# A router of sixteen columns turned round, and a hand-written front put in a new order

## The reference

```python
x = x + attention(layernorm(x), ctx)          # q, k, v projections with biases, softmax over 375 rows
h = layernorm(x)
router_probs = softmax(h @ w_router)          # 8 experts
gate_weights = softmax(h @ w_gating / 0.1)
cw = router_probs * gate_weights
cw = cw / (sum(cw) + 1e-9)
out = x + sum over e of cw[e] * ((silu(h @ w_gate[e]) * (h @ w_up[e])) @ w_down[e])   # 256 -> 1024 -> 256
```

## Time and profile before

| | |
|---|---|
| median of 3 runs | 981.25 us (980.57 to 981.32) |
| profiled execution, its own time | 981.21 us |
| its span | 979.4 us |
| instructions | 16,565 |
| TensorE busy | 971.5 us |
| VectorE, ScalarE, GpSimd busy | 745.7, 482.9, 671.1 us |
| mean granted TensorE clock | 0.999 |

### The profile page before, as it was taken

One profiled execution on the slowest core, in us unless ns is written; L12 is line 12 of the kernel. 1 busy time (PEld: TensorE's weight loads), 2 busy tenths in 40 slices (PEclk: granted clock), 3 DMA queues, 4 the chain that ended last, 5 costly groups with the idle time before them and its releaser, 6 DMA issues.

```text
span 979.4 us, 16565 instructions
## 1 busy us (share of the span) xinstructions
PE 971.5 (99%) x6193; PEld 927.3 (95%) x6193; DVE 745.7 (76%) x1353; ACT 482.9 (49%) x853; POOL 671.1 (69%) x514
## 2 busy tenths in 40 slices
PE   8999999999999999999999999999999999999998
PEld 7999999999999999999999999999999999999998
DVE  6987446877778777788777887777877778777785
ACT  6897554454444444544535444444445454444441
POOL 4799876776757676667667675766766676757642
PEclk9999999999999999999999999999999999999999
DMA  9250140010001010010101010010101010100002
GB/s 227 81 152 20 49 143 23 22 44 16 29 22 44 23 36 30 22 45 22 44 2 43 23 44 22 22 44 23 44 22 32 13 45 22 44 22 23 1 1 76
DMA packets 37352, 40.63 MB, mean 41 GB/s; under 512 B 2644, under 2 KB 35272, under 8 KB 37272
## 3 DMA queue, kind: packets, MB, share of 16 engines
q1 hardware_dynamic: 37264, 39.58, 13.6%
q10 hardware_dynamic: 8, 0.00, 0.0%
HBM read 35.90 MB, written 3.67 MB: 40 GB/s over the span
## 4 chain that ended last, share of the span: by engine, by line
PE 97%; DMA 2%; ACT 0%; SPq 0%; POOL 0%; issue 0%; DVE 0%; DVEq 0%
PE ps L272 94%; DMA shared<-in_ctx 1%; PE ps L1527 1%; PE ps L1615 1%; DMA xf<-in_L_xattn_Wk 1%; PE ps L1555 0%; PE ps L1602 0%; PE ps L1572 0%; PE ps L1516 0%; POOL arena L413 0%; SPq L286 0%; DVE xsacc L1236 0%; ACT arena L647 0%; ACT arena L701 0%; PE ps L1473 0%
## 5 line engine op out<-in xcount | busy, mean ns | idle before, releaser
L272 PE MATMUL ps<-arena 128*128 128x256 f32 (+4 forms) x3120 | 413.7, 284 | 0.2
L272 PEld LDWEIGHTS ps<-arena 128*128 128x128 f32 (+2 forms) x3120 | 403.2, 189 | 6.3 <-POOL arena L480 0.2
L480 POOL TENSOR_TENSOR arena<-shared,arena 128x448 fp32r<-128x448 f32 x196 | 251.0, 1294 | 191.4 <-ACT arena L808 185.6
L272 PE MATMUL ps<-xc_hi,w_hi 128*128 128x448 f32 x904 | 331.9, 367 | 0.0
L272 PE MATMUL ps<-xc_hi,w_lo 128*128 128x448 f32 x904 | 330.2, 365 | 0.0
L272 PE MATMUL ps<-xc_lo,w_hi 128*128 128x448 f32 x904 | 329.7, 365 | 0.0
L801 ACT ACTIVATE shared<-shared 128x448 f32<-128x448 f32 x180 | 101.4, 579 | 192.0 <-DVE shared L1176 125.0
L272 PEld LDWEIGHTS ps<-xc_hi,w_lo 128*128 128x128 f32 x904 | 169.8, 188 | 13.8
L272 PEld LDWEIGHTS ps<-xc_hi,w_hi 128*128 128x128 f32 x904 | 170.6, 189 | 10.2
L272 PEld LDWEIGHTS ps<-xc_lo,w_hi 128*128 128x128 f32 x904 | 170.6, 189 | 10.1
L1170 DVE TENSOR_TENSOR shared<-ps,shared 128x448 f32<-128x448 f32 x60 | 37.5, 625 | 110.8 <-PE ps L272 110.8
(11 more groups left out here) (145 smaller groups left out, 1098.7 us busy)
## 6 DMA issues: line engine op xcount, KB each, us to landing
early<-in_L_ffn_w_down SPq DMA_DIRECT2D x16, 512.0 KB, 4.0
shared<-in_ctx SPq DMA_DIRECT2D x16, 336.0 KB
w_raw<-in_L_ffn_w_gate SPq DMA_DIRECT2D x17, 256.0 KB, 2.9
w_raw<-in_L_ffn_w_up SPq DMA_DIRECT2D x17, 256.0 KB, 3.2
early<-in_L_ffn_w_gate SPq DMA_DIRECT2D x15, 256.0 KB, 2.8
early<-in_L_ffn_w_up SPq DMA_DIRECT2D x15, 256.0 KB, 3.1
x_dram<-xsacc SPq DMA_DIRECT2D x8, 224.0 KB, 3.7
xsacc<-x_dram SPq DMA_DIRECT2D x1, 1792.0 KB, 7.6
```

The lines of the kernel that those rows point to most:

```text
L272: ins = nc.tensor.matmul(dst, w, m, start=first and i == 0, stop=last and i == len(passes) - 1, skip_group_check=onto)
L480: nc.gpsimd.tensor_tensor(h[:, 1, j, at:at + TC], tile, h[:, 0, j, at:at + TC].bitcast(fp32), ALU.subtract).then_inc(hid_lo_done, 1)
```

## The change

The router is computed the other way round. `split_router` (new, VectorE) splits the 16 columns into a high and a low part of fp32r, which lie side by side as 32 columns. `route(cp, c)` (four calls in place of fourteen) takes these 32 columns as the stationary operand and streams a row of 448 tokens past them, for the two halves of the inputs and for `xc_hi` and `xc_lo`: four passes. The result is 32 x 448 in bank 3 or 4. `keep_routed` (new, ScalarE) copies it to SBUF (into a part of `up_t` not yet in use), `transpose_logits(cp)` (new, TensorE) turns it back in seven 128-token pieces to bank 5, and `keep_logits` adds up the part from the high and the part from the low weights. The waits on `logits_done` in `values`, `transpose_norm2` and `down` go; `keep_norm2(4)` no longer waits for `logits_ready`, and the first `quad` waits for both logits.

Beside this, the lists of all five engines before the first `quad` are written in a new order. Nothing is added or taken away there but the router's parts; ten fillers stay ten, placed otherwise: eight before `transpose_weights(1)` where there were five, none in the stretch to `mix_ctx(0)` where there were four, then two where there was one.

```diff
+        wr_split = sb("wr_split", [P, DK, 2, 2 * E], fp32r)
+        lt = up_t[0:4 * E, 0:2, :]
-        ps_l = ps[:, X2_BANK, 0:RT * 2 * E].rearrange("p (i n) -> p i n", i=RT)
+        ps_lt = [ps[0:4 * E, 3 + c, 0:TC] for c in range(2)]
+        ps_l = ps[:, 5, 0:RT * 4 * E].rearrange("p (i l n) -> p i l n", i=RT, l=2)
...
+            load_x(0)
             load_weights(0)
-            load_x(0)
             load_weights(1)
+            load_x(1)
             load_ctx_half(0, 0)
-            load_x(1)
+            load_ctx_half(0, 1)
+            load_router()
             load_wv()
-            load_ctx_half(0, 1)
             load_ctx_half(1, 0)
             load_x(2)
+            load_set(0)
+            load_ctx_half(1, 1)
+            load_ctx(2, 0)
+            load_bv()
             load_x(3)
-            load_ctx_half(1, 1)
-            load_bv()
-            load_set(0)
-            load_ctx(2, 0)
             load_ctx(2, 1)
             load_ctx(3, 0)
+            load_set(1)
...
+            def keep_routed(cp, c):
+                sc.wait_ge(lt_ready, 2 * cp + c + 1)
+                if cp == 0:
+                    sc.wait_ge(cn_lo_done, 2 * PAIRS)
+                else:
+                    sc.wait_ge(logits_ready, 1)
+                nc.scalar.copy(lt[:, c, :], ps_lt[c]).then_inc(lt_kept, 1)
...
# ScalarE's list
             weights_high(0)
+            norm1(0)
             weights_high(1)
-            norm1(0)
+            xt_high(0)
             ct_high(0, 0)
-            xt_high(0)
             cn_high(0, 0)
             m_high()
             ct_high(0, 1)
+            cn_high(0, 1)
             q_high(0)
+            cn_high(1, 0)
             norm1(1)
-            cn_high(0, 1)
+            high_set(0)
             xt_high(1)
+            ct_high(1, 0)
             wv_high()
-            cn_high(1, 0)
-            ct_high(1, 0)
             exponentials(0, 0)
...
# VectorE
+                nc.vector.tensor_reduce(logits[:, cp * RT:(cp + 1) * RT, :], ps_l.rearrange("p i l n -> p i n l"),
+                                        AX.X, ALU.add).then_inc(logits_done, 1)
+            def split_router():
+                ve.wait_ge(router_in, 2 * DMA)
+                nc.vector.tensor_copy(wr_split[:, :, 0, :], wr_raw[:]).then_inc(wr_hi_done, 1)
+                ve.wait_ge(wr_hi_done, 1)
+                low(wr_split[:, :, 1, :], wr_raw[:], wr_split[:, :, 0, :]).then_inc(wr_done, 1)
...
+            stats1(0)
             split_biases()
-            stats1(0)
             weights_low(0)
+            stats1(1)
             weights_low(1)
-            stats1(1)
...
# TensorE
+            def route(cp, c):
+                pe.wait_ge(wr_done, 1)
+                pe.wait_ge(part_lo[cp, "first" if c == 0 else "second"], 1)
+                if (cp, c) == (1, 1):
+                    pe.wait_ge(second7_lo, 1)
...
+                accumulate(ps_lt[c], [(wr_split[:, k - 1, :, :].rearrange("p l n -> p (l n)"), x[:, cp, PLAIN_A[c + 1, k], :])
+                                      for k in (1, 2) for x in (xc_hi, xc_lo)]).then_inc(lt_ready, 1)
+            def transpose_logits(cp):
+                pe.wait_ge(lt_kept, 2 * (cp + 1))
...
+                for i in range(RT):
+                    ins = nc.tensor.transpose(ps_l[:, i, :, :].rearrange("p l n -> p (l n)"), lt_f[:, i * P:(i + 1) * P], ident[0:4 * E, 0:4 * E])
...
             queries(0)
             transpose_ctx(1, 0)
+            scores(0, 0)
             transpose_norm(1)
-            keep_busy(1)
-            scores(0, 0)
             scores(0, 1)
             queries(1)
             transpose_probs(0, 0)
             transpose_ctx(1, 1)
-            keep_busy(1)
-            keep_busy(1)
-            keep_busy(1)
+            scores(1, 0)
             transpose_probs(0, 1)
-            scores(1, 0)
             transpose_ctx(2, 0)
```

More of the change, by code:

```diff
@@ L842, in _ @@
             q_high(2)
+            pt_high(1, 0)
+            norm1(3)
             pt_high(1, 1)
-            norm1(3)
-            high_set(0)
-            ct_high(3, 0)
             at_high(0)
             xt_high(3)
+            cn_high(2, 0)
+            ct_high(3, 0)
+            exponentials(2, 0)
             cn_high(2, 1)
-            cn_high(3, 0)
[L851 to L858, removed]
+            high_set(1)
+            pt_high(2, 0)
+            normalise(1)
+            ct_high(3, 1)
+            q_high(3)
+            exponentials(2, 1)
+            at_high(1)
+            pt_high(2, 1)
+            norm1(4)
+            cn_high(3, 0)
             ct_high(4, 0)
+            cn_high(3, 1)
             xt_high(4)
-            cn_high(3, 1)
-            at_high(1)
+            exponentials(3, 0)
             normalise(2)
-            exponentials(3, 0)
             ct_high(4, 1)
-            cn_high(4, 0)
+            exponentials(3, 1)
             q_high(4)
-            exponentials(3, 1)
             pt_high(3, 0)
@@ L871, in _ @@
             pt_high(3, 1)
-            at_high(2)
+            cn_high(4, 0)
             cn_high(4, 1)
@@ L902, in _ @@
             at_high(4)
-            keep_norm2(2)
             ct_high(7, 0)
             high_part(0, "first")
+            keep_norm2(2)
+            exponentials(6, 0)
+            exponentials(6, 1)
             normalise(5)
+            xt_high(7)
+            pt_high(6, 0)
             cn_high(7, 0)
-            exponentials(6, 0)
-            xt_high(7)
-            exponentials(6, 1)
+            pt_high(6, 1)
+            at_high(5)
+            q_high(7)
             keep_norm2(3)
-            at_high(5)
@@ L913, in _ @@
             high_part(0, "second")
[L914 to L918, removed]
             ct_high(7, 1)
             cn_high(7, 1)
+            high_part(0, "s13")
             exponentials(7, 0)
+            high_part(0, "s2")
             exponentials(7, 1)
+            plain_silu(0, 0)
+            plain_silu(0, 1)
             pt_high(7, 0)
-            normalise(6)
-            pt_high(7, 1)
@@ L926, in _ @@
[L926 to L930, removed]
             plain_high(0, 0)
             plain_high(0, 1)
+            pt_high(7, 1)
+            plain_silu(0, 2)
+            normalise(6)
+            at_high(6)
+            keep_norm2(4)
+            normalise(7)
             plain_high(0, 2)
-            normalise(7)
             plain_silu(0, 3)
+            plain_high(0, 3)
+            plain_silu(1, 0)
@@ L1280, in _ @@
             both_biases()
+            ct_low(0, 1)
             times_bk(0)
-            ct_low(0, 1)
             q_low(0)
@@ L1793, in _ @@
             transpose_ctx(5, 0)
+            transpose_mix(2)
             scores(4, 0)
@@ L1810, in _ @@
             mix_ctx(4)
             transpose_probs(5, 0)
+            transpose_norm2(1)
             transpose_ctx(6, 1)
+            queries(6)
             transpose_probs(5, 1)
-            queries(6)
             values(3)
             transpose_ctx(7, 0)
+            scores(6, 0)
             transpose_mix(4)
-            scores(6, 0)
+            scores(6, 1)
             transpose_norm2(2)
             mix_ctx(5)
-            scores(6, 1)
+            transpose_norm(7)
+            transpose_probs(6, 0)
@@ L1822, in _ @@
+            transpose_ctx(7, 1)
+            transpose_probs(6, 1)
+            transpose_mix(5)
             values(4)
-            transpose_norm(7)
-            transpose_ctx(7, 1)
-            transpose_probs(6, 0)
+            queries(7)
             transpose_norm2(3)
-            transpose_mix(5)
-            queries(7)
-            transpose_probs(6, 1)
-            route(0, 0)
-            route(0, 1)
-            route(0, 2)
-            route(0, 3)
             mix_ctx(6)
             scores(7, 0)
-            route(0, 4)
@@ L1852, in _ @@
             plain(0, 0, 3)
+            transpose_mix(6)
+            transpose_norm2(4)
             mix_ctx(7)
+            values(6)
+            transpose_mix(7)
             plain(0, 1, 3)
-            transpose_mix(7)
             plain(1, 0, 0)
+            route(0, 0)
             transpose_norm2(5)
             plain(1, 1, 0)
+            plain(1, 0, 1)
             values(7)
-            plain(1, 0, 1)
-            transpose_norm2(6)
             plain(1, 1, 1)
             plain(1, 0, 2)
+            route(0, 1)
```

325 lines of the change are left out of this document (156 added, 169 removed).

## The result

The changed kernel takes 983.38 us (median of 12 executions, 980.55 to 985.79), the kernel before 980.86 (12, 980.20 to 982.50). The ratio is 1.0023, with an interval of 1.0012 to 1.0033: slower by 2.5 us where 2.0 faster had been forecast, and outside the range of 977.5 to 981.7. The profiled execution took 983.63 us with a span of 981.8, against 981.21 and 979.4; what follows compares these two.

What follows compares the result with a forecast made beforehand. TensorE was taken as the bound, full from 36.3 us, with the front deciding when that run begins. 981.2 - 1.2 (router) - 0.7 (front) = 979.3, shaded to 979.2 us; range 977.5 to 981.7.

Steps and rivals of the forecast that it cites:

- The step that failed: VectorE in the front: two 32-column router-weight splits cost some 0.3 us together, off the path if the order holds.
- Theory A: From the experiments' expectations: VectorE's 3.56 us subtraction, both inputs in SBUF, is held by GpSimd's SBUF work; this sets the end.
- the rival in which the gap closes: Front: the awaited landing was the true cause and VectorE keeps up; 2.0 us less, 978.0 us; chance 0.20.
- Term 1, the router: TensorE: 5.89 us of old products replaced by 16 passes (3.33) and 14 transposes (1.43); 1.2 us less.
- Term 2, the front: Stretch up to mix_ctx(1): new orders bring the context block of pair 2 earlier, ending at 39.15, not 39.87; 0.7 us less.
- the walk: Front, step by step: x(1) 7.8 us, merged product 10.4, first scores 17.1, weight set 18.1, transpose_ctx(2, 0) 25.9.
- ScalarE waits for the weight set: Front: high_set(0) holds xt_high(1), ct_high(1, 0) and first exponentials behind a landing; at 23 us, 984.2 us; chance 0.12.
- The front gives nothing: Front: late merged product and longer ScalarE list eat the earlier block, leaving the router's gain; 980.0 us; chance 0.20.
- A new wait in the laced stage: keep_routed late, or transpose_mix(7) too close behind mix_ctx(7); about 1 us each, 980.5 to 981.5 us; chance 0.10.
- The 5.4 us: Router's 32-byte rows in the first burst: 512 packets at 10.5 ns, making 984.4 us; the forecast took 0.1 instead.
- the signs named for a wrong prediction: high_set(0) DMA wait of 2 us or more; 32-column transposes at 0.04; TensorE idle over 1 us between 40 and 130.
- the signs named for a right one: Passes near 0.208 us, transposes 0.1; transpose_ctx(2, 0) near 25.9, released by VectorE; merged product 10.4; no TensorE gap after 36.

Runs made afterwards that it cites:

- experiment 1: Changed kernel with split_router moved earlier in VectorE's list, to about 16.8 us, where GpSimd is idle; 979.72 us, ratio 0.9988.
- experiment 2: Changed kernel with the router weights' subtraction on GpSimd behind cn_low(1, 1), the cast staying on VectorE; 979.20 us, ratio 0.9982.
- 11: Changed kernel with the router split off VectorE: cast on ScalarE, subtraction on GpSimd; 980.05 us, ratio 0.9987.
- 7: Changed kernel with router weights first copied to PSUM by ScalarE, VectorE splitting them from there at the same place; 980.02 us, ratio 0.9993.
- experiment 10: Changed kernel with GpSimd waiting for wr_done ahead of cn_low(1, 1), a pause between its two context splits; 981.44 us, ratio 1.0004.
- experiment 3: Changed kernel with five more TensorE fillers ahead of transpose_ctx(2, 1), VectorE's stall left as it is; 983.02 us, ratio 1.0014.
- experiment 9: Changed kernel repeated as it is, against the kernel before; 983.75 us, ratio 1.0027.
- experiment 5: Kernel before, in its own orders, with only the router turned round and its split on ScalarE and GpSimd near 100 us; 980.88 us, ratio 1.0004.
- 8: The kernel of experiment 2 without the two fillers beside transpose_probs(1, 1); 979.51 us, ratio 0.9986.
- experiment 6: Changed kernel's new orders in all lists, with the old router near its former places and no weight split; 989.19 us, ratio 1.0097.
- 12: Repeat of experiment 3, the changed kernel with five fillers in TensorE's gap, beside experiment 9; 983.71 us, ratio 1.0026.
- experiment 4: The kernel of experiment 1 with high_set(0) moved behind exponentials(0, 0) on ScalarE; 980.53 us, ratio 0.9999.

## Why the prediction was wrong

**The step that failed** is the sentence on "two splits of 32 columns in the front, some 0.3 us together", with "Nothing of this is on the path if the order holds". Both halves are wrong. Alone the two take 0.17 + 0.19 = 0.36 us (experiment 1), so the estimate would have been good for an idle GpSimd. In their place in the list they take 4.3 us (0.71 + 3.56), because GpSimd is at work in SBUF from 25.8 to 31.8 without a pause. Theory A is shown from four sides: another time (1), another engine (2, 11), another source (7), and half the GpSimd work (10). The second half fails as VectorE is the engine that sets the front's pace from 27 us to 37 (the chain of experiment 3). The prediction had counted it as busy for 24.6 of 29.5 us and used that only against the rival in which the gap closes. On an engine so full an added instruction needs a price even where it runs at its full pace: the 0.36 us of experiment 1 at 17 us moved `queries(1)` by 0.42 us against the first scores (3.38 us behind them, 2.96 in experiment 2).

In size: the front lost 3.85 us where a gain of 0.7 stood in the sum, and the stretch behind it gained 1.49 where 1.2 stood. Together that is 3.85 + 0.7 - 0.29 = 4.3 us, and the median lies 4.2 above the forecast. How much of it is the split on VectorE shows best between the profiles of experiments 9 and 11, which neither waited for the weight set nor fell to the lower clock in the front: the long run begins at 130.24 and at 126.64, 3.6 us apart.

The trace of before already held a sign that was not read. Two subtractions of 128 x 224, both inputs in SBUF, with GpSimd at work beside the first (VectorE's timeline, GpSimd's, and the per-line view of the second):
```profile
129.25 1.92 DVE L1246 TENSOR_TENSOR lg<-logits,lg_top 128x224 f32<-128x224 f32 x1
```
```profile
128.53 2.40 POOL L474 TENSOR_TENSOR arena<-early,arena 128x1024 fp32r<-128x1024 f32 x1
```
```profile
L1254 DVE TENSOR_TENSOR lg<-lg,lg_top x1: 393/393/393, 133.0 to 133.0; 128x224 f32<-128x224 f32 x1
```
L1246 takes 1.92 us and ends behind the GpSimd instruction (131.17 and 130.93); L1254, of the same size and with GpSimd idle, takes 0.39. The Trainium skill has the rule (SBUF — State Buffer, Who interferes with whom): "A DVE instruction with two SBUF inputs contends with a GpSimd instruction that reads SBUF", since they share a port pair, whoever is first has it for the whole instruction, and a cast can fall under it too. The trace agrees: 3.56 us against 0.19, and 0.19 with one input in PSUM.

**Term 1, the router (-1.2 us forecast).** Right in kind, a little more in size: 1.49 us. The passes took 0.204 each (16 in 3.27 us; 0.208 taken), the transposes 7 in 0.54 us, 0.077 each, where 0.1 had been taken; 5.89 - 3.27 - 1.08 = 1.54. The argument that such work "counts one for one" was too simple: in the old order the same router gives nothing (experiment 5).

**Term 2, the front (-0.7 us forecast).** It is worth nothing that can be told from the spread. Without the stall the front ends at 39.87 (1), 39.72 (2), 40.10 (7), 39.11 (8) and 39.51 (11); with the old orders it ends at 39.87 (before) and 39.47 (5); 39.15 had been forecast. The first steps of the walk held: the statistics of x(1) began at 7.87 (7.8 forecast), the merged product at 10.01 (10.4), the first scores at 16.95 (17.1). `transpose_ctx(2, 0)` no longer waited for a transfer, as forecast, but began at 26.32 and not at 25.9, later than the 26.23 of before. Off were the weight set, 18.57 in place of 18.1, and VectorE behind it. From 26 us on the walk followed TensorE alone and expected the gaps behind to close.

**The rivals.** "ScalarE waits for the weight set" had the right sign, and the wait is there, but it is small: 0.81 us in the changed kernel's profile, 0.50 to 0.70 in three others (6, 7, 12) and none in the rest. It cost up to 0.9 us at `transpose_ctx(2, 0)`, and the loss stays without it: experiment 9 has none and still takes 983.0 in its profiled execution. "The front gives nothing" describes the kernel once the split is out of the way: 980.0 had been given for it, and 979.20 to 980.05 were measured (1, 2, 7, 8, 11). "A new wait in the laced stage" did not come: TensorE is full from 40.15 us to 130.86. The router's 32-byte rows landed 5.6 to 6.9 us after issue and nothing waited for them. The 5.4 us that were worked out by the floor in the Trainium skill (DMA: Bandwidth & Descriptors, Bandwidth) are not to be seen. The page has that floor for a 4 KB transfer issued by GpSimd; these rows were issued by SyncE. Of the signs named for a wrong prediction none appeared; the fault was in an edit that none of them watched. Of the signs named for a right one, the release of `transpose_ctx(2, 0)` by VectorE did not come.

**What a better version gives.** Experiments 1, 2, 8 and 11 beat both kernels, by 0.7 to 1.5 us against before: 979.20 to 980.05. Their intervals overlap, so none of them is shown best. In profiled executions the long run begins 1.5 to 1.8 us earlier than at 128.48; the medians show less, in part because the profiled execution of before (981.21) was itself above its medians of 980.5 to 980.9.

**What stays open.** The changed kernel's executions spread widely (980.55 to 985.79). The shortest ones, near 981, all have a mean clock of 1.000; the eleven of its 19 below that have a median of 983.6, the other eight 982.3. Yet with fillers that hold the clock (17 executions of experiments 3 and 12) the medians are 983.0 and 983.7, and three of the 17 are near 981 as well. What makes the short ones short is not known; VectorE may get its turn between GpSimd's instructions in them, but no profile fell on one, and this is not shown. What the new orders of the front would do with the old router was not isolated: experiment 6 met another wait first.

## What to carry to other kernels

Price an added VectorE instruction by where its inputs lie and by what GpSimd does at that moment, not by its size: with all of its inputs in SBUF beside a busy GpSimd it lasted here until GpSimd paused, so put it where GpSimd is idle, feed it from PSUM, or give it to another engine. If an instruction of before takes five times as long as its twin in the same trace, find out why before the change is priced. And treat slow work behind a gap with suspicion: if another queue sets the pace, clock or gap given back turns into the next wait (0.3 us of 1.9 here); if none does, it costs in full (experiment 4).

## What was not expected of the hardware

GpSimd instructions back to back gave VectorE no turn between them. The subtraction was issued at 28.3 us, one `cn_low` would have let it go near 29.9, and it ended at 31.83 behind the second. A pause between the two (experiment 10) let it go at 29.87. The cast showed the same in each of the seven profiles in which it ran from SBUF beside `low_set(0)` (experiments 2, 3, 8, 9, 10, 12 and the changed kernel): it took 0.45 to 1.03 us in place of 0.17, and each time ended within 0.1 us of that instruction's end. And a gap of near 2 us of TensorE brought its clock from 2.4 to 1.2 GHz in one execution (1.84 us idle) and not in another of the same kernel (1.98 us idle); in experiment 4 a gap of 1.75 us did. What it cost depended on what was late behind the gap: 0.3 us where VectorE was, 1.2 us where nothing was.
